# Building a 0/1 count matrix on the chip: lists loaded for two buckets at once, ranges opened by their first product, one-hots in four register-addressed slots

## The reference

```python
x = layernorm(x + L0(x, edges))   # two APPNP hops, then two matrix products
x = layernorm(x + L1(x, edges))   # hypergraph: node -> hyperedge (2500 of them) -> node
x = layernorm(x + L2(x, edges))   # weighted sparse sum over source and target
x = layernorm(x + L3(x, edges))   # edge attention with a softmax over all edges
```

## Time and profile before

| what | us |
|---|---|
| median of the timed runs | 7867.82 |
| lowest and highest of them | 7810.16, 7903.07 |
| the profiled execution's own time | 7873.77 |
| its span in the trace | 7872.0 |
| stage that builds the matrix (1734 to 2583 us of the span) | 849 |

### The profile page before, as it was taken

One profiled execution on the slowest core, in us unless ns is written; L12 is line 12 of the kernel. 1 busy time (PEld: TensorE's weight loads), 2 busy tenths in 40 slices (PEclk: granted clock), 3 DMA queues, 4 the chain that ended last, 5 costly groups with the idle time before them and its releaser, 6 DMA issues. The chain is left out here.

```text
span 7872.0 us, 98123 instructions
## 1 busy us (share of the span) xinstructions
PE 3812.2 (48%) x16163; PEld 2422.8 (31%) x16164; DVE 3389.4 (43%) x11703; ACT 1127.3 (14%) x3853; POOL 3603.0 (46%) x3613
## 2 busy tenths in 40 slices
PE   1600150016666775775945554333333356666665
PEld 0300030001111342443423332232322256665663
DVE  4946370026666444114021113333333555665666
ACT  0000000001111000002000001000000244444443
POOL 0045777710000684660056664666666155555550
PEclk9999999987777896887955555555555578888886
DMA  9411111261111563652711111111111233333332
GB/s 129 72 30 36 48 42 53 53 23 78 75 78 73 202 210 106 220 168 87 274 43 45 45 45 42 45 44 43 44 44 44 48 95 95 95 98 95 95 98 35
DMA packets 674873, 648.60 MB, mean 82 GB/s; under 512 B 495848, under 2 KB 564441, under 8 KB 655638
## 3 DMA queue, kind: packets, MB, share of 16 engines
q1 hardware_dynamic: 546182, 379.55, 18.1%
q0 software_dynamic: 128384, 266.34, 12.2%
q10 hardware_dynamic: 144, 1.28, 0.0%
HBM read 502.61 MB, written 144.27 MB: 82 GB/s over the span
## 5 line engine op out<-in xcount | busy, mean ns | idle before, releaser
L828 POOL DMA_INDIRECT bucketed_edges<-edge_rows,idx x784 | 817.6, 1043 | 784.0 <-issue 725.3
L483 POOL DMA_INDIRECT gathered<-node_table,idx x576 | 624.4, 1084 | 1130.7 <-ACT idx L471 958.4
L1337 POOL DMA_INDIRECT gathered<-node_table_xq,idx x832 | 796.3, 957 | 752.8 <-issue 223.7
L359 POOL DMA_INDIRECT gathered<-node_table,idx x816 | 772.7, 947 | 495.9 <-issue 249.8
L374 PE MATMUL ps<-onehots,gathered 128*128 128x128 f32 x1632 | 430.6, 443 | 846.7 <-DVE agg L402 609.0
L663 POOL DMA_INDIRECT gathered<-node_table,idx x588 | 556.1, 946 | 330.7 <-issue 171.7
L430 PE MATMUL ps<-gathered,junk 128*128 128x512 f32 x1182 | 622.4, 636 | 125.7 <-DMA gathered<-edge_counts 125.6
L678 PE MATMUL ps<-onehots,gathered 128*128 128x128 f32 x1176 | 467.7, 501 | 409.3 <-DMA gathered<-node_table,idx 394.9
L374 PEld LDWEIGHTS ps<-onehots,gathered 128*128 128x128 f32 x1632 | 365.1, 327 | 912.2 <-issue 834.3
L1177 PE MATMUL ps<-onehots 128*128 128x512 bf16 x1152 | 472.4, 487 | 187.0 <-DVE onehots L1204 183.9
L678 PEld LDWEIGHTS ps<-onehots,gathered 128*128 128x128 f32 x1176 | 294.6, 311 | 582.4 <-DMA gathered<-node_table,idx 559.4
(11 more groups left out here) (373 smaller groups left out, 6729.2 us busy)
## 6 DMA issues: line engine op xcount, KB each, us to landing
gathered<-edge_counts SPq DMA_DIRECT2D x99, 1280.0 KB
edge_counts<-gathered SPq DMA_DIRECT2D x49, 1280.0 KB
gathered<-node_table,idx POOLq DMA_INDIRECT x1980
bucketed_edges<-edge_rows SPq DMA_DIRECT2D x52, 544.0 KB, 12.5
edge_rows<-bucketed_edges SPq DMA_DIRECT2D x208, 128.0 KB
gathered<-edge_counts SPq DMA_DIRECT2D x48, 512.0 KB
side_rows<-edge_counts SPq DMA_DIRECT2D x48, 512.0 KB
edge_rows<-in_edge_attr_dram SPq DMA_DIRECT2D x108, 128.0 KB
```

Of the source, the lines that this page charges most:

```text
L359: nc.gpsimd.indirect_dma_start(g[:, k, :], None, table, bass.IndirectOffsetOnAxis(m.idx[:, k:k + 1], 0)).then_inc(S["landed"][k], 16)
L483: nc.gpsimd.indirect_dma_start(g[:, k, :], None, a.table, bass.IndirectOffsetOnAxis(m.idx[:, k:k + 1], 0)).then_inc(S["landed"][k], 16)
L828: nc.gpsimd.indirect_dma_start(a.bucketed, bass.IndirectOffsetOnAxis(m.idx[:, k:k + 1], 0), m.erow[:, k, :], None).then_inc(S["scattered"] ...
L1337: nc.gpsimd.indirect_dma_start(g[:, k, :], None, a.table2, bass.IndirectOffsetOnAxis(m.idx[:, k:k + 1], 0)).then_inc(S["landed"][s], 16)
```

## The change

It does three things, in the two functions.

- **Lists.** The nine integers of a bucket are laid out as six (first tile and pairs of each range) and three (pairs before). After bucket 0, DVE and PE load 18 integers once for an odd and the next even bucket, at the start of a turn of the walk. Each range has at least two pairs of tiles (a floor of 3 tiles before halving).
- **Opening.** PE no longer opens a block with a product by zero. The first pair of a range stands ahead of the loop, and the product of its first tile has `start=True`; the loop runs from pair 1. PE waits for `emptied` of all blocks of the range at once.
- **Slots.** There are four slots for one-hots instead of two, in another buffer (`m.pads`). Their addresses are no longer fixed: slot = (number of the pair) % 2 * 2, plus 0 or 1 for the tile. So the two writes of DVE and both operands of PE's product have an address from registers.

```diff
--- before.py
+++ after.py
@@ -45,6 +45,8 @@
 KW = NK * KB
 PARTS = ((0, 1), (1, 3), (3, 5))
 NR = len(PARTS)
+ROWL = 3 * NR
+SLOTS = 4
 WB = KB * max(b - a for a, b in PARTS)
 SPLIT = (E - (P - 1) * NT) // U
 DUMP = BT * P
@@ -1043,8 +1045,7 @@
     inb, rev, fwd, f = (m.gather[0:NB, k * BT:(k + 1) * BT] for k in range(4))
     one, two = m.gather[:, 4 * BT:5 * BT], m.gather[:, 5 * BT:6 * BT]
     first, past = m.lists[PB, 0:NR + 1], m.lists[PB, 6:7 + NR]
-    rowF = m.gather[0:1, 6 * BT:6 * BT + 3 * NB * NR]
-    three = rowF.rearrange("p (b k c) -> p b k c", k=NR, c=3)
+    rows = m.gather[0:1, 6 * BT:6 * BT + ROWL * NB].rearrange("p (b c) -> p b c", c=ROWL)
     pairs, ends = (m.gather[0:1, 7 * BT + j * NB * NR:7 * BT + (j + 1) * NB * NR] for j in range(2))
     halves = lambda t: t.rearrange("p (h t) -> p h t", h=2)
     with phase(nc, "lists", "dve cmp marked counted taken listed rows") as (S, block):
@@ -1075,18 +1076,21 @@
             step(V.tensor_scalar(first, first, -1.0, float(BT), ALU.mult, ALU.add))
             step(V.tensor_scalar(first, first, float(BT - 1), None, ALU.min))
             step(V.tensor_tensor(past, past, first, ALU.subtract))
-            V.tensor_scalar(past, past, 1.0, None, ALU.max).then_inc(S["listed"], 1)
+            step(V.tensor_scalar(past[:, 0:NR], past[:, 0:NR], 3.0, None, ALU.max))
+            V.tensor_scalar(past[:, NR:NR + 1], past[:, NR:NR + 1], 1.0, None, ALU.max).then_inc(S["listed"], 1)
             v.wait_ge(S["rows"], 2 * NR)
+            table = m.startI[0:1, 0:ROWL * NB].rearrange("p (b c) -> p b c", c=ROWL)
+            by_bucket = lambda t: t.rearrange("p (b k) -> p b k", k=NR)
             for q in range(NR):
-                step(V.tensor_copy(three[:, :, q, 0], m.ps[0:1, 5, q * NB:(q + 1) * NB]))
-                step(V.tensor_scalar(three[:, :, q, 1], m.ps[0:1, 5, (NR + q) * NB:(NR + q + 1) * NB], 1.0, None, ALU.add))
-            step(V.tensor_copy(m.startI[0:1, 0:3 * NB * NR], rowF))
-            step(V.tensor_scalar(m.startI[0:1, 0:3 * NB * NR].rearrange("p (i c) -> p i c", c=3)[:, :, 1],
-                                 m.startI[0:1, 0:3 * NB * NR].rearrange("p (i c) -> p i c", c=3)[:, :, 1], 1, None, ALU.arith_shift_right))
-            step(V.tensor_copy(pairs, m.startI[0:1, 0:3 * NB * NR].rearrange("p (i c) -> p i c", c=3)[:, :, 1]))
+                step(V.tensor_copy(rows[:, :, 2 * q], m.ps[0:1, 5, q * NB:(q + 1) * NB]))
+                step(V.tensor_scalar(rows[:, :, 2 * q + 1], m.ps[0:1, 5, (NR + q) * NB:(NR + q + 1) * NB], 1.0, None, ALU.add))
+            step(V.tensor_copy(table[:, :, 0:2 * NR], rows[:, :, 0:2 * NR]))
+            for q in range(NR):
+                step(V.tensor_scalar(table[:, :, 2 * q + 1], table[:, :, 2 * q + 1], 1, None, ALU.arith_shift_right))
+                step(V.tensor_copy(by_bucket(pairs)[:, :, q], table[:, :, 2 * q + 1]))
             step(V.tensor_tensor_scan(ends, m.ones[0:1, 0:1].to_broadcast([1, NB * NR]), pairs, 0.0, ALU.mult, ALU.add))
             step(V.tensor_tensor(ends, ends, pairs, ALU.subtract))
-            step(V.tensor_copy(m.startI[0:1, 0:3 * NB * NR].rearrange("p (i c) -> p i c", c=3)[:, :, 2], ends))
+            step(V.tensor_copy(table[:, :, 2 * NR:], by_bucket(ends)))
 
         @block.tensor
         def _(pe):
@@ -1110,9 +1114,12 @@
 def build_counts(nc, m, a):
 
     rows = [m.gather[:, e * KW:(e + 1) * KW] for e in range(2)]
-    low = m.oh[:, :, :].rearrange("p t n -> p (t n)").bitcast(BF16)
-    ohd = [low[:, e * WB:(e + 1) * WB] for e in range(2)]
-    ohs = [low[:, 2 * WB + e * P:2 * WB + (e + 1) * P] for e in range(2)]
+    low = m.pads[:, :].bitcast(BF16)
+    ohd, ohs = low[:, 0:SLOTS * WB], low[:, SLOTS * WB:SLOTS * (WB + P)]
+
+    def slot(pair):
+
+        return nc.s_assert_within(pair % 2 * 2, 0, 2, skip_runtime_bounds_check_because="twice a rest of two")
     iotaI = m.hid[:, :, :].rearrange("p t d -> p (t d)").bitcast(I32)[:, 0:WB]
     iotaK = m.junk[:, :, :].rearrange("p t d -> p (t d)").bitcast(FP16)[:, 0:WB]
     zeros = m.zerob[:, 0:1].to_broadcast([P, KB])
@@ -1125,14 +1132,23 @@
                 body(eng.snap(i * 2 + 1), 1, i)
                 body(eng.snap(i * 2 + 2), 0, i + 1)
 
-        def lists(eng, engine, b):
-
-            got = nc.values_load_multi_w_load_instructions(m.startI[0:1, bass.ds(b * (3 * NR), 3 * NR)], engines=[engine])[1]
-            return [got[3 * k:3 * k + 3] for k in range(NR)]
-
-        def bounded(eng, before):
-
-            return eng.snap(nc.s_assert_within(before, 0, NK * (BT + NB)))
+        def walk_lists(eng, engine, body):
+
+            def load(b, n):
+                got = nc.values_load_multi_w_load_instructions(m.startI[0:1, bass.ds(b * ROWL, n * ROWL)], engines=[engine])[1]
+                return [got[ROWL * k:ROWL * (k + 1)] for k in range(n)]
+            body(0, load(0, 1)[0])
+            with eng.Fori(0, (NB - 1) // 2) as i:
+                b = eng.snap(i * 2 + 1)
+                odd, even = load(b, 2)
+                body(b, odd)
+                body(eng.snap(i * 2 + 2), even)
+
+        def parts(eng, row):
+
+            bounded = lambda x: eng.snap(nc.s_assert_within(x, 0, NK * (BT + NB)))
+            for k, (k0, k1) in enumerate(PARTS):
+                yield k0, k1, row[2 * k], row[2 * k + 1], bounded(row[2 * NR + k])
 
         @block.sync
         def _(sp):
@@ -1159,26 +1175,27 @@
         @block.tensor
         def _(pe):
             T = nc.tensor
-            pe.sem_inc(S["used"], 2)
+            pe.sem_inc(S["used"], SLOTS)
             pe.sem_inc(S["emptied"], NK)
 
-            def body(b, e, u):
-                at = lists(pe, mybir.EngineType.PE, b)
-                for r, (k0, k1) in enumerate(PARTS):
-                    for k in range(k0, k1):
-                        pe.wait_ge(S["emptied"], b * NK + k + 1)
-                        T.matmul(m.ps[:, k, :], m.zerob[:, :], zeros, start=True, stop=False)
-                    n, before = at[r][1], bounded(pe, at[r][2])
-                    with pe.Fori(0, n) as j:
-                        c = pe.snap((before + j) * 2)
+            def body(b, row):
+                for k0, k1, lo, n, before in parts(pe, row):
+                    def pair(p, first):
+                        c, at = pe.snap(p * 2), pe.snap(slot(p))
                         for h in range(2):
                             pe.wait_ge(S["ready"], c + (h + 1))
                             for k in range(k0, k1):
-                                last = T.matmul(m.ps[:, k, :], ohs[h], ohd[h][:, (k - k0) * KB:(k - k0 + 1) * KB], start=False, stop=False)
+                                last = T.matmul(m.ps[:, k, :], ohs[:, bass.ds(at * P + h * P, P)],
+                                                ohd[:, bass.ds(at * WB + h * WB + (k - k0) * KB, KB)],
+                                                start=first and h == 0, stop=False)
                             last.then_inc(S["used"], 1)
+                    pe.wait_ge(S["emptied"], b * NK + k1)
+                    pair(pe.snap(before), True)
+                    with pe.Fori(1, n) as j:
+                        pair(pe.snap(before + j), False)
                     for k in range(k0, k1):
                         T.matmul(m.ps[:, k, 0:1], m.zerob[:, :], m.zerob[:, 0:1], start=False, stop=True).then_inc(S["summed"], 1)
-            walk(pe, body)
+            walk_lists(pe, mybir.EngineType.PE, body)
 
         @block.vector
         def _(v):
@@ -1189,22 +1206,20 @@
             v.wait_ge(S["iota"], 1)
             step(V.tensor_copy(iotaK, iotaI))
 
-            def body(b, e, u):
-                at = lists(v, mybir.EngineType.DVE, b)
-                for r, (k0, k1) in enumerate(PARTS):
+            def body(b, row):
+                for k0, k1, lo, n, before in parts(v, row):
                     w = (k1 - k0) * KB
-                    lo, n, before = at[r][0], at[r][1], bounded(v, at[r][2])
                     with v.Fori(0, n) as j:
-                        c = v.snap((before + j) * 2)
-                        t = v.snap(nc.s_assert_within(lo + j * 2, 0, BT, skip_runtime_bounds_check_because="a list ends at the last tile"))
+                        c, at = v.snap((before + j) * 2), v.snap(slot(before + j))
+                        t = v.snap(nc.s_assert_within(lo + j * 2, 0, BT + 2, skip_runtime_bounds_check_because="a list ends at the last tile"))
                         for h in range(2):
                             v.wait_ge(S["used"], c + (h + 1))
-                            V.tensor_scalar(ohs[h], m.iotab[:, :], m.meta[:, bass.ds(t + h, 1), 2], m.bF[:, bass.ds(b, 1)],
+                            V.tensor_scalar(ohs[:, bass.ds(at * P + h * P, P)], m.iotab[:, :], m.meta[:, bass.ds(t + h, 1), 2], m.bF[:, bass.ds(b, 1)],
                                             ALU.subtract, ALU.is_equal)
-                            V.tensor_scalar(ohd[h][:, 0:w], iotaK[:, 0:w], m.meta[:, bass.ds(t + h, 1), 1], -float(k0 * KB),
```

(3 more changed lines are left out.)

## The result

The changed kernel takes **8146.93 us** (median of four runs, 8101.86 to 8183.55), the kernel before 7875.76 us (four runs). The ratio is 1.0365, 95% interval 1.0327 to 1.0402: slower, inside the forecast range and 50 us over the point (8097). Between the two medians lie 271 us, where the forecast had 230. The profiled execution after took 8163.63 us, its span is 8161.8.

A forecast was written before the change was run, and what follows sets the result against it. DVE's sequencer was taken to bound the stage. Addresses +247, removed waits -28, loads +10 and table +1 made +230 us on 7873.8, 8104, given as 8097 us since the median is 6 lower; range 7930 to 8215.

The forecast's parts named there:

- What bounds the stage: In the 849 us stage, DVE's sequencer, doing register arithmetic for addresses, sets the pace for most of its 361 pairs.
- Four addresses a pair, 0.72 narrow and 0.66 wide: DVE's one-hots need four more register addresses a pair, 0.18 us each, 0.06 hidden in wide pairs: +247 us.
- loses PE's name: Expected sign: DVE's idle time before L1202, the wide one-hots, no longer ends with PE, and grows.
- The loads, +10: Joint loads of 18 unaligned integers on DVE take 4.08 us each, 24 times, in place of single-bucket loads: +10 us.
- The opening, 0 by itself: Dropping PE's 245 products by zero, 101.4 us busy, gains 0 more, since PE waits for DVE anyway.
- The -28 for waits: DVE's waits for PE in middle ranges (23 us) and in steps out of them (5 us) go: -28 us.
- The 12 us of narrow pairs in even buckets: 47 narrow pairs taking 2.06 instead of 1.81 us, unrelated to slots; left standing, could go or come with loop places.
- faster: Rival: with four tiles of lead, address arithmetic runs beside DVE's engine, pairs fall towards busy time: 7731 us; chance 0.14.
- the cheap one: Rival: low price for DVE's new addresses, with quick or slow list loads: 7936 to 8004 us; chance 0.12.
- fetch of code: Rival: the walk's longer loop makes DVE fetch its code anew, 24 x 3 us, +72: 8169 us; chance 0.10.
- TensorE as the bound: Rival: PE's operand addresses make wide pairs up to 3.0 us instead of 2.47, +86: 8183 us; chance 0.08.
- TensorE's products wait for its own arithmetic: Sign of a wrong prediction: PE's first products wait on "issue", taken as its own arithmetic, rather than on DVE.

The follow-up runs named there:

- d2: b1 with the slot addresses computed from registers on DVE alone, still the same two slots, 11 integers loaded: stage 1064.0 us.
- b2: b1 with targets and sources copied once into planes and the bucket's column copied once a bucket: stage 728.1 us, whole 0.9838 of before.
- e1: Kernel before with only the four register-addressed slots added, on both engines: stage 1068.3 us.
- e4: Kernel after with table rows of 12 integers, so each joint load begins at a multiple of 16 bytes: stage 1025.6 us.
- b1: Kernel after with two fixed slots, rows of 12 integers and one bucket's list a load: stage 816.0 us, whole 0.9946 of before.
- b3: b2 with the four register-addressed slots on both engines: stage 905.2 us, whole 1.0068 of before.
- e6: Kernel before with ranges opened by their first product, one wait for all blocks and lists of at least three: stage 860.0 us against 852.0.
- b4: b2 with ranges opened by products with zeros again: stage 724.9 us against 728.1, whole 0.9870 of before.
- e2: Kernel after with two slots at fixed addresses again, joint load and opening kept: stage 919.0 us.
- d1: b1 with the slot addresses computed from registers on TensorE alone, still the same two slots, 11 integers loaded: stage 1028.1 us.
- l1: Kernel after with DVE's joint loads ahead of even buckets and TensorE's ahead of odd ones: stage 1171.0 us.

## Why the prediction was right, step by step

**What bounds the stage** was read rightly: DVE's sequencer, in the kernel after in all pairs. DVE's addresses alone make 226 us and its pairs of 2.52 (d2); cheaper ones give 88 back (b2).

**Four addresses a pair, 0.72 narrow and 0.66 wide.** The pairs went from 1.81 to 2.52: 0.71, narrow and wide alike. The choice of 0.18 an address held as a sum, and not in its parts. I had four new records of 0.139 us and 0.04 for each handover. There are five a pair, (3964 - 2152) / 361, which add 226.7 / 361 = 0.63 us, 0.126 each; of the 0.71 that leaves 0.08, or 0.016 a handover. One record too few and too much for each came out even, and this is luck. That 0.06 would be hidden in wide pairs did not hold, and the idle time before L1219 is 106.2 us where I said 60. The term, with the waits it takes away, was 247 - 28 = 219 us; e1 measured 216, e4 against b1 210. Middle ranges stood at 2.16 and came to 2.5, 0.35 and not 0.71 more: there is the gain from removed waits. But the sign "loses PE's name" failed: TensorE ends 167.3 us of the idle time before L1217, where it was 93.2. That it does not set the pace all the same is read from d2 and b3, not from this view.

**The loads, +10: mis-sized.** DVE's loads went from 86.3 to 119.7 us, +33. The step that failed is the straight line through one and nine integers, at 0.222 for each further one, which gave 4.08 us for 18; 4.91 was measured, so the second nine cost 0.31 each. The direction (never a multiple of 16 bytes, so never quick) was right, and more lay in it than its term said: e4 took 80 us back with it. The Trainium skill (Runtime: NRT & Kernel Launch, Instruction fetch mechanics) states about 200 ns per register even in bulk; it speaks of the loads ahead of a kernel. The runs here agree for no length exactly: 18 unaligned are 0.27 each on DVE and 0.35 on TensorE, 21 aligned ones 0.08 each.

**The opening, 0 by itself.** It is +8 on the kernel before (e6) and +3 on b4 (b2), each between two single executions. The -28 for waits was put down to the slots and to the opening products both; e2 and e6 show that without the slots the middle ranges stay at 2.2, so the slots alone remove them.

**The 12 us of narrow pairs in even buckets** (2.06 for 1.81): they did come back, but a like effect appeared in the middle ranges of odd buckets, 2.78 us for 2.52 in 32 steps, 8 us, with 0.12 in 24 steps out of them, 3 us. I had let them stand; the net is about nothing. In d2, where TensorE has no address arithmetic for the slots, these steps take 2.77 us too, so the cause is on DVE's side: the extra time stands in two gaps between records of its sequencer, some 0.12 us ahead of the last record of a L1219 and as much behind the loop's branch. Whether the loops' places in the code make it stays open.

**The table, +1:** the list stage went from 56.1 to 57.2.

Summed from the runs: the slots are 216 (e1). Between e1 and the kernel after, which differ by the loads and the opening, lie 37.5 us, and 33.4 of them are DVE's loads. The 4 that are left hold the opening and the loops' places together (the middle ranges of odd buckets alone take 2.50 us in e1 and 2.78 after, 9 us); e6's +8 was measured with two slots, where wide pairs wait for TensorE, and need not be the same with four. The forecast for the stage was 229 (the table's 1 lies outside): the loads were 23 more, the slots 3 less, the rest 4 more. The remaining 36 of the profiled difference are not in this stage.

**The rivals.** The arithmetic was not free beside the engine (faster): pairs rose by 0.71. The order of time with the sequencer's records says how. The arithmetic of an L1219 begins 0.02 us after the L1217 ahead of it has started (2005.59 and 2005.56 in the kernel after), so it does run beside the engine, but one instruction ahead and no more, and the sequencer's time for a pair is the longer of the two. That is also why a wide pair is no longer than a narrow one and nothing more was hidden in it. The price was not the cheap one. No fetch of code is seen: the stage has one packet on each of the two instruction queues, before as after, where the attention loop had 125:

```profile
q8 instruction: 1, 0.02, 0.0%
q14 instruction: 1, 0.01, 0.0%
```

And from bucket to bucket DVE is idle for 6.19 us around a load of 4.91, 1.28 more, where it was 3.16 around 2.08, 1.08 more. TensorE as the bound fell by d2, by b3 and by narrow pairs that take as long as wide ones (that rival's sum took 0.4 us a pair; its own 3.0 - 2.47 is 0.53, or 114 us and a time of 8211, still in the range). But its arithmetic, which I costed at nothing under cover, costs up to 190 us with two slots (d1), and the lead of four hides it. I had also said that the prediction is wrong if TensorE's products wait for its own arithmetic. 186.2 us of "issue" are there, but 112.0 of them stand behind its own joint loads, and 74.2 elsewhere; with quick loads (e4) 52.2 are left in all, and the pairs are the same. So the sign was badly chosen: "issue" holds register loads too, and both were harmless, since with four slots TensorE still keeps up with what DVE delivers. The slots hide a cost that they bring themselves.

## What to carry to other kernels

Where an engine's sequencer sets the pace, an operand at an address from a register can cost its arithmetic at every use, as it did here, and a longer ring of buffers addressed so can cost more than the waits it removes; count the records, on both sides of the ring. Before a load into registers is made longer, look at where it begins: in these runs as many integers cost two to three times as much off a multiple of 16 bytes. Cutting address work that is already there (planes instead of a stride of three, a column copied to a fixed place) was worth 88 us in this stage, three times what the removed waits had promised.

## What the runs showed of the hardware

- Loads of integers into registers, on DVE (aligned: beginning at a multiple of 16 bytes): aligned, 9 in 0.86 us, 11 in 1.31, 18 in 1.59, 21 in 1.62; unaligned, 9 in 2.08 and 18 in 4.92 (6.27 in e2). On TensorE 18 unaligned took 6.35 us. Neither series is a straight line. Set apart, 18 unaligned integers took both engines as long as with an overlap of 3.3 us (l1 and after); in e2, with 5.6 us of overlap, DVE took 6.27.
- Register arithmetic on DVE's sequencer: five records more a pair, 0.63 us in sum, made the pair 0.71 us longer (b1 and d2, before and after), although DVE computes for only 1.34 (narrow) to 1.60 us (wide) of the 2.52. The records of an instruction begin 0.02 us after the start of the one ahead (after, 2005.56).
- Products with zeros in TensorE's idle time went with a higher granted clock: 0.75 against 0.67 (before, e6) and 0.77 against 0.72 (b4, b2), and with products of 487 and 478 ns in place of 548 and 515. In this stage it bought nothing net; each figure is from one profiled execution.
- The clock's column is a mean over the window and did not always go with the products: e4 had 0.72 granted and 610 ns, the kernel after 0.52 and 608, with the same pairs of 2.52 us.

```profile
1799.27:2824.89 1025.62, 624.14 (x1372) 149.68 (x1397) 540.24 (x1446) 134.00 (x245) 0.98 (x1) 0.72 0.15 63
...
L1189 PE MATMUL ps<-attend_slots 128*128 x1127 | 620.9, 610 | 400.9 <-DVE attend_slots L1220 256.3 <-ACT gathered L1173 78.8 <-issue 52.2
```
